# A batch attention with its next group's scores issued a step sooner, its reciprocals kept in the queries' PSUM bank, and VectorE's work in each step put in another order

## The chip, the cores and the metric

The kernel runs on one core of a Trainium2 chip. The metric is the device time of one execution in microseconds (us). All data are float32. The engines are named as in the profile: PE is TensorE (matmuls), DVE VectorE, ACT ScalarE, POOL GpSimd and SP SyncE, which here issues DMAs only. Each engine works through its own instructions in order; semaphores order the engines among themselves.

## What is computed

Two transformer-like layers over x of 16 batches, 512 tokens, 128 features. Layer 0 is a linear attention and a token-shift feed-forward, layer 1 a retention and then the block that the change is in:

```python
def _mha(x, Wqkv, bqkv, Wo, bo):          # S = 16 (batches), B = 512 (tokens)
    qkv = x @ Wqkv.T + bqkv               # 4 heads of 32
    scores = einsum('bhqd,bhkd->bhqk', q, k) * (1.0 / sqrt(hd))
    att = softmax(scores, axis=-1)
    o = einsum('bhqk,bhkd->bhqd', att, v)
    return o.transpose(2, 0, 1, 3).reshape(S, B, D) @ Wo.T + bo

def _moe(x, Wg, W1, b1, W2, b2):          # 8 experts, 128 -> 512 -> 128
    idx = argmax(xf @ Wg.T, axis=-1)
    ...
y = _layer_norm(x + _mha(x, Wqkv, bqkv, Wo, bo), g1, be1)
z = _layer_norm(y + _moe(y, Wg, W1, b1, W2, b2), g2, be2)
```

The attention runs across the 16 batches, for each of the 512 token positions by itself. A token then goes to the one expert of eight whose logit is largest.

## The kernel before

`kernel` calls `build`, which runs six stages one after the other: `prologue`, `attention` (layer 0), `token_shift_ffn`, `attention` (layer 1), `attend_and_route` and `run_experts`. A stage is a block with one program for each engine, and a stage begins when the one before has ended on all engines. The change is in `attend_and_route` alone. There the 8192 rows are 16 groups g of 4 tiles of 128 rows (`G` = 16). Every engine runs `step(s)` for s from -4 to 20 (`run`), written out in full, and in a step each engine works on groups at different stages. The work of a group g:

- ACT normalises it (`act_xn`, in step g-4), POOL scales and shifts it (`pool_scale`, `pool_h`, step g-4) and adds a bias for the residual (`pool_xb`, step g-3), three instructions on 128x512 each. PE transposes it (`pe_T`, step g-3) and ACT brings that to SBUF (`act_hT`).
- PE makes queries, keys and values (`pe_qk`, `pe_v`, step g-2), into the PSUM banks `pq`, `pk` and part of `rows_ps`. ACT takes them out (`act_q`, `act_k`, `act_v`). SP sends the keys to a layout by heads (`sp_kx`, four DMAs).
- `pe_scores` (step g) puts the scores into the bank `pS`: first a mask (L1320), then 32 small matmuls (L1327). DVE takes the maximum (`vec_max`, L1334), subtracts it (`vec_shift`, L1339), ACT makes the exponential (`act_exp`, L1345, in its step behind `act_q` and `act_k` of group g+2), and DVE sums it (`vec_total`, L1350), makes reciprocals (`vec_reciprocal`, L1357), multiplies (`vec_probs`, L1362) and transposes in blocks (`vec_transpose`, L1369, tile `pc`). The reciprocals `rc` are the first 16 columns of `pS`, and the routing's scratch (`lg`, `first`) lies in `pS` too: so `pe_scores(g)` waits for the probabilities of g-1 (`pn_ready`) and for routing.
- SP sends the transposed probabilities to another layout (`sp_ax`, four DMAs into `ax`). In step g+1 PE makes the values' sums (`pe_values`, L1388, bank `pO`), ACT takes them out (`act_o`), and PE multiplies by the output weights (`pe_out`, L1405, in `rows_ps`).
- In step g+2 DVE adds the residual (`vec_u`, L1414) and takes the router's logits (`vec_logits`, L1421), then statistics of the rows (`vec_stats`: four L1429 and the copy L1430 of 128x4 place numbers) and `vec_var` (four L1437).
- In every even step 2r+4 DVE chooses the experts of two groups (`vec_choose`, L1459 to L1468), PE ranks them (`pe_rank`, end of its step), and in step 2r+5 DVE makes the rows' addresses (`vec_dest`, L1485 to L1494). In step g+5 POOL scatters the group's rows by address (`pool_row`, four indirect DMAs, L1512), and it needs these addresses for that.

The order of an engine's step is written out by hand in `pe_step`, `act_step`, `vec_step` and `pool_step`. Before the change, PE's step s is: scores(s), queries, keys and values of s+2, values(s-1), transposition of s+3, out(s-1), ranking. DVE's step s is: rows and logits, statistics of s-2, addresses (odd steps), maximum and subtraction of s, `vec_var`, some statistics of x in the first steps, choice (even steps), then sum, reciprocals, probabilities and transposition of s. In the last steps (s of 12 and more) POOL has no more groups to prepare, and `pool_step` places waits between its rows: for scores(s), for values(s-1) and for out(s-1). Below, "scores(g)", "values(g)", "out(g)" stand for `pe_scores`, `pe_values`, `pe_out` of group g. The functions as they are, with the line numbers of the profile:

## Time and profile before

| what | us |
|---|---|
| median of 3 runs | 1056.25 |
| lowest, highest of them | 1048.0, 1058.28 |
| the profiled execution | 1047.97 |
| its span in the trace | 1046.2 |
| PE, DVE, POOL, ACT, PEld busy in the span | 860.2, 867.7, 721.6, 631.7, 618.0 |

The trace covers one execution. Its span leaves 1.8 us of the device time outside. PEld is the loading of weights, which lies beside PE's matmuls. `attend_and_route` takes from about 684 us of the span to about 875. A row of a timeline gives the start, the duration of the merged instructions, the engine, the line and operation, output and inputs, the count, and in brackets how long the engine was idle before it and what ended that. A window gives the busy time of each engine in a stretch.

### The profile page before, as it was taken

What the parts mean: (1) busy time and instruction counts of PE and PEld (TensorE: products, weight loads), DVE (VectorE), ACT (ScalarE), POOL (GpSimd) and SP (SyncE); (2) the same over time, 40 slices, a digit from 0 to 9 for tenths busy, and PEclk for the clock granted to TensorE, in tenths of its full rate; (3) what the DMA queues carried; (4) which work ended last, traced back from release to release, by engine and by line L of the source; (5) the groups of instructions that cost most, each with busy time, mean ns of one, the idle gap of its engine ahead of it and who ended that gap; (6) DMA issues with size and microseconds to landing.
All of it is one profiled execution on the core that took longest, in us unless ns stands there. A gap on an engine that the chain in (4) does not pass through costs nothing. (4 is left out here: it accounts for less than half of the span.)

```text
span 1046.2 us, 25423 instructions
## 1 busy us (share of the span) xinstructions
PE 860.2 (82%) x5240; PEld 618.0 (59%) x5240; DVE 867.7 (83%) x2853; ACT 631.7 (60%) x1636; POOL 721.6 (69%) x626
## 2 busy tenths in 40 slices
PE   5799999999968867989898989558888732999993
PEld 5466666666636644555555555335555532999993
DVE  5589999999976976989898989778899761899995
ACT  2555555555438956676767675467665202999992
POOL 4488888888852218999999999665598461355554
PEclk9899999999989989999999999869999755999997
DMA  9520000000000000000000000254576664544420
GB/s 245 164 69 1 0 0 0 0 0 0 1 4 1 0 1 1 11 20 10 20 10 20 10 20 10 67 153 110 158 213 205 186 221 124 146 129 132 133 65 20
DMA packets 64935, 70.11 MB, mean 67 GB/s; under 512 B 8965, under 2 KB 52178, under 8 KB 64740
## 3 DMA queue, kind: packets, MB, share of 16 engines
q1 hardware_dynamic: 50612, 47.20, 16.2%
q0 software_dynamic: 6368, 16.89, 4.7%
q10 hardware_dynamic: 7872, 5.08, 1.8%
q8 instruction: 32, 0.52, 0.2%
q14 instruction: 51, 0.42, 0.1%
HBM read 32.32 MB, written 24.50 MB: 54 GB/s over the span
## 5 line engine op out<-in xcount | busy, mean ns | idle before, releaser
L473 PE MATMUL a_pS<-a_kv,utri 128*128 128x360 f32 (+3 forms) x768 | 264.9, 481 | 19.4 <-POOL a_kv L464 9.7
L464 POOL TENSOR_TENSOR a_kv<-a_qk,a_vv 128x1152 f32<-128x1152 f32 (+1 forms) x128 | 264.2, 2065 | 12.6 <-DVE a_qk L438 12.6
L473 PEld LDWEIGHTS a_pS<-a_kv,utri 128*128 128x128 f32 x768 | 136.3, 191 | 100.8 <-issue 25.3
L569 POOL TENSOR_TENSOR a_tt<-a_tt 128x576 f32<-128x576 f32 (+1 forms) x128 | 156.9, 1226 | 49.9 <-DVE a_tt L553 46.0
L553 DVE TENSOR_TENSOR a_tt<-a_pS,a_qk 128x360 f32<-128x360 f32 (+3 forms) x384 | 181.0, 526 | 11.3 <-PE a_pS L473 8.3
L1930 POOL DMA_INDIRECT out_dram<-x_o,x_place x71 | 69.1, 973 | 78.6 <-DVE x_o L1917 75.9
L581 DVE TENSOR_REDUCE a_nd<-a_tt 128x144 f32<-128x720 f32 (+3 forms) x128 | 104.5, 816 | 0.0
L519 ACT ACTIVATE a_tt<-a_pI 128x144 f32<-128x144 f32 (+1 forms) x96 | 40.1, 417 | 105.5 <-PE a_pI L481 105.4
L512 PEld LDWEIGHTS a_pO<-wgate,a_yT 128*128 128x128 f32 x256 | 44.8, 193 | 75.2 <-issue 36.6
L1512 POOL DMA_INDIRECT ys<-m_S,m_dest x64 | 63.0, 984 | 36.8 <-issue 12.3
L512 PE MATMUL a_pO<-wgate,a_yT 128*128 (+1 forms) x256 | 54.7, 296 | 30.8 <-POOL a_yT L543 22.6
L1868 PE MATMUL x_pZ<-w,x_hT 128*128 x568 | 76.9, 279 | 1.4 <-issue 1.3
L1819 ACT ACTIVATE x_w<-w 128x644 f32 x71 | 52.4, 741 | 31.3 <-PEq L1651 26.3
L1868 PEld LDWEIGHTS x_pZ<-w,x_hT 128*128 128x128 f32 x568 | 69.9, 194 | 2.1 <-issue 1.9
L410 ACT ACTIVATE a_vv<-a_pQ 128x128 f32<-128x128 f32 x122 | 33.8, 277 | 55.3 <-PE a_pQ L401 53.4
L372 ACT ACTIVATE a_xn<-X,nmr,rstd 128x128 f32 (+1 forms) x128 | 60.9, 485 | 2.0 <-DVE nmr L275 1.8
L287 DVE BATCH_NORM_STATS2 bn<-X 128x6 f32<-128x128 f32 (+1 forms) x256 | 57.4, 278 | 1.1 <-DMA X<-xs 0.9
L401 PE MATMUL a_pQ<-W,a_hT 128*128 128x384 f32 x122 | 51.5, 504 | 4.2 <-ACT a_hT L388 2.7
L456 POOL TENSOR_TENSOR a_qk<-a_ra,a_rb 128x256 f32<-128x256 f32 x64 | 47.0, 735 | 8.7 <-DVE a_rb L449 8.7
L401 PE MATMUL a_pQ<-wqkv,a_hT 128*128 128x384 f32 x122 | 50.3, 494 | 1.5 <-ACT a_hT L388 1.5
L481 PEld LDWEIGHTS a_pI<-a_R,a_qT 128*128 128x128 f32 x192 | 34.4, 189 | 28.4 <-ACT a_qT L525 11.3
L1850 ACT ACTIVATE x_hT<-x_pA,x_w 128x128 f32<-128x128 f32 x142 | 43.9, 362 | 9.4 <-PE x_pB L1842 9.4
(298 smaller groups left out, 2192.8 us busy)
## 6 DMA issues: line engine op xcount, KB each, us to landing
x_yl<-ys SPq DMA_DIRECT2D x71, 193.5 KB, 2.4
X<-xs SPq DMA_DIRECT2D x16, 256.0 KB, 5.4
kx<-m_kc SPq DMA_DIRECT2D x64, 64.0 KB
ax<-m_pc SPq DMA_DIRECT2D x64, 64.0 KB
m_S<-X SPq DMA_DIRECT2D x16, 256.0 KB, 3.1
xs<-X SPq DMA_DIRECT2D x15, 256.0 KB
w<-in_L_ffn_W_dram SPq DMA_DIRECT2D x1, 2048.0 KB
m_S<-gw ACTq DMA_DIRECT2D x6, 256.0 KB, 3.0
```

The costliest lines, as they stand in the source:

```text
L287: v.bn_stats(K.bn[:, ds(n, 1), :].rearrange("p a f -> p (a f)"), x[:, ds(n, 1), :].rearrange("p a f -> p (a f)"))\
L372: act.activation(xn[:, t, :], tile(K.X, 4 * b + t), ACT.Identity, bias=column(K.nmr, 4 * b + t), scale=column(K.rstd, 4 * b + t)).then_inc ...
L401: pe.matmul(bank_of(b, t, start)[:, 0:3 * P], hT[:, t * P:(t + 1) * P], wqkv, start=True, stop=True).then_inc(qkv_ps, 1)
L464: pool.tensor_tensor(kv[:, t % 2, :, :, :], kk.unsqueeze(2).to_broadcast([P, H, J, D]), vv[:, t, :, :].unsqueeze(3).to_broadcast([P, H, J, ...
L473: pe.matmul(pS[c][:, 0:(h1 - h0) * SC], K.utri[:, :], flat[:, h0 * SC:h1 * SC], start=True, stop=True).then_inc(u_done, 1)
L512: pe.matmul(pO[:, 0:P], yT[:, :], tile(K.wgate[:, 0 if layer == 0 else 2, :, :], b), start=True, stop=True).then_inc(proj_ps, 1)
L553: v.tensor_tensor(tt[:, t % 2, h0:h1, :, 0:D], pS[c][:, 0:(h1 - h0) * SC].rearrange("p (h j i) -> p h j i", i=D, j=J), q[:, h0:h1, :].unsq ...
L569: pool.tensor_tensor(tt[:, t % 2, :, :, D // 2:D], tt[:, t % 2, :, :, D // 2:D], tt[:, t % 2, :, :, 0:D // 2], ALU.add).then_inc(half_done, 1)
L581: v.tensor_reduce(nd[:, t % 2, :, :], tt[:, t % 2, :, :, D // 2:rows], AX.X, ALU.add).then_inc(red_done, 1)
L1512: pool.indirect_dma_start(out=A["ys"], out_offset=bass.IndirectOffsetOnAxis(ap=dest[:, g // 2 % 2, at:at + 1], axis=0), in_=S[:, 4 * (g % ...
L1868: mm = pe.matmul(pZ[j % 2][:, 0:P], hT[:, j % 2, c * P:(c + 1) * P], K.w2[:, ds(e, 1), c, :].rearrange("p a f -> p (a f)"), start=(c == 0) ...
L1930: pool.indirect_dma_start(out=token_rows, out_offset=bass.IndirectOffsetOnAxis(ap=place[:, j:j + 1], axis=0), in_=o[:, j % 4, :], in_offse ...
```

## The change

In `attend_and_route`:

- `rc` moves from `pS` to the first 16 columns of `pq`. `pe_qk(g)` waits for `pn_ready` of g-2 (the probabilities of group g-3 made), `pe_scores(g)` for `sm_ready` of g (the subtraction of g-1 done) where it waited for `pn_ready`, and `vec_reciprocal(g)` for the queries up to g+2 to be taken out of `pq`, where it waited for `sm_ready` and `hot_ready`.
- PE issues scores(s+1) in step s, behind the transposition of s+3 and ahead of out(s-1). It issued scores(s) first in step s.
- DVE begins its step with the maximum and subtraction, then rows and logits, then in odd steps (and the first and last ones) statistics, variance and addresses. In the even steps 4 to 14 statistics and variance come last, behind the transposition.
- In POOL's last steps the second row waits for values(s-1), the third for scores(s+1), the fourth for out(s-1) as before.

```diff
--- before.py
+++ after.py
@@ -1146,7 +1146,8 @@
         pv, pU = four(512 - 3 * PE_), four(1024 - PE_)
         pos, sums = rows_ps[:, 0:8 * E].rearrange("p (e n) -> p e n", e=E), rows_ps[:, 8 * E:9 * E]
 
-        rc, lg, first = pS[:, 0:16], pS[:, 64:64 + 8 * E].rearrange("p (n e) -> p n e", e=E), pS[:, 128:136]
+
+        rc, lg, first = pq[:, 0:16], pS[:, 64:64 + 8 * E].rearrange("p (n e) -> p n e", e=E), pS[:, 128:136]
         unit = lambda g: g // 2 if g < G - 2 else g - G // 2 + 1
         groups = lambda r: [2 * r, 2 * r + 1] if r < G // 2 - 1 else [r + G // 2 - 1]
         tiles = lambda r: 4 * len(groups(r))
@@ -1272,6 +1273,7 @@
         def pe_qk(pe, g):
             pe.wait_ge(hT_ready, g + 1)
             wait(pe, q_ready, g)
+            wait(pe, pn_ready, g - 2)
             pe.matmul(pq[:, :], K.W[:, W_FQ, :], hT[:, :], start=True, stop=True).then_inc(q_ps, 1)
             wait(pe, kc_ready, g)
             pe.matmul(pk[:, :], K.W[:, W_FK, :], hT[:, :], start=True, stop=True).then_inc(k_ps, 1)
@@ -1315,7 +1317,7 @@
 
             if g == 0:
                 pe.wait_ge(mask_ready, 1)
-            wait(pe, pn_ready, g)
+            wait(pe, sm_ready, g)
             wait(pe, hot_ready, (g - 3) // 2)
             pe.matmul(pS[:, :], mask[:, 0:P], mask[:, P:].unsqueeze(1).to_broadcast([2, 16, 32]), start=True, stop=False,
                       skip_group_check=True)
@@ -1352,8 +1354,7 @@
         def vec_reciprocal(v, g):
             v.wait_ge(sum_ready, g + 1)
             wait(v, pn_ready, g)
-            v.wait_ge(sm_ready, g + 1)
-            wait(v, hot_ready, (g - 2) // 2)
+            v.wait_ge(q_ready, min(g + 3, G))
             v.reciprocal(rc, sm_sum[:, :]).then_inc(rc_ready, 1)
 
         def vec_probs(v, g):
@@ -1521,8 +1522,6 @@
 
 
         def pe_step(pe, s):
-            if there(s):
-                pe_scores(pe, s)
             if there(s + 2):
                 pe_qk(pe, s + 2)
                 pe_v(pe, s + 2)
@@ -1530,6 +1529,8 @@
                 pe_values(pe, s - 1)
             if there(s + 3):
                 pe_T(pe, s + 3)
+            if there(s + 1):
+                pe_scores(pe, s + 1)
             if there(s - 1):
                 pe_out(pe, s - 1)
             if even(s - 4) and s < G:
@@ -1576,17 +1577,18 @@
 
         def vec_step(v, s, link):
 
-            if there(s - 2):
-                vec_u(v, s - 2)
-                vec_logits(v, s - 2)
-                vec_stats(v, s - 2)
-            if even(s - 5) and s < G:
-                vec_dest(v, link, (s - 5) // 2)
+            late = even(s - 4) and s < G
             if there(s):
                 vec_max(v, s)
                 vec_shift(v, s)
             if there(s - 2):
+                vec_u(v, s - 2)
+                vec_logits(v, s - 2)
+            if there(s - 2) and not late:
+                vec_stats(v, s - 2)
                 vec_var(v, s - 2)
+            if even(s - 5) and s < G:
+                vec_dest(v, link, (s - 5) // 2)
             x_stats(v, s)
             if s in PARTS:
                 v.wait_ge(stats, 4 * (PARTS[s][2] - 2))
@@ -1598,6 +1600,9 @@
                 vec_reciprocal(v, s)
                 vec_probs(v, s)
                 vec_transpose(v, s)
+            if late:
+                vec_stats(v, s - 2)
+                vec_var(v, s - 2)
             if s in PARTS:
                 vec_x_offset(v, *part_of(s))
             if s == G or s == G + 1:
@@ -1612,12 +1617,12 @@
             if s >= G - 4:
                 if there(s - 5):
                     pool_row(pool, s - 5, 0)
-                pool.wait_ge(s_ps, min(s + 1, G))
                 if there(s + 3):
                     pool_xb(pool, s + 3)
                 if there(s - 5):
+                    pool.wait_ge(o_ps, min(s, G))
                     pool_row(pool, s - 5, 1)
-                    pool.wait_ge(o_ps, min(s, G))
+                    pool.wait_ge(s_ps, min(s + 2, G))
                     pool_row(pool, s - 5, 2)
                     pool.wait_ge(w_ps, min(s, G - 1))
                     pool_row(pool, s - 5, 3)
```

## Rows read from the trace of the kernel before

**Rows 1.** Windows of the span: busy us by engine, then TensorE's clock, DMA share, GB/s

```profile
core 0: us, PE busy (x) PEld busy (x) DVE busy (x) ACT busy (x) POOL busy (x), PEclk, DMA share, GB/s
...
745.90:806.90 61.00, 51.52 (x639) 35.44 (x637) 55.07 (x163) 38.61 (x79) 54.96 (x49) 1.00 0.68 205
...
806.90:845.30 38.40, 27.31 (x324) 21.25 (x325) 30.85 (x119) 10.13 (x20) 19.77 (x20) 0.72 0.61 188
```

**Rows 2.** Timeline of POOL: start us, us, what; idle before and its releaser in brackets

```profile
745.87 1.19 POOL L1512 DMA_INDIRECT ys<-m_S,m_dest  x1 [7.64 <-DVE m_dest L1492]
...
760.73 1.28 POOL L1258 TENSOR_TENSOR X<-X,m_gb 128x512 f32<-128x512 f32 x1
...
763.47 0.97 POOL L1512 DMA_INDIRECT ys<-m_S,m_dest  x1 [0.31 <-issue]
...
806.94 0.97 POOL L1512 DMA_INDIRECT ys<-m_S,m_dest  x1 [0.30 <-issue]
...
844.09 0.97 POOL L1512 DMA_INDIRECT ys<-m_S,m_dest  x1 [1.06 <-PE m_pO L1388]
...
865.80 0.97 POOL L1512 DMA_INDIRECT ys<-m_S,m_dest  x1 [0.30 <-issue]
```

**Rows 3.** Timeline of DVE, the odd step 7 and the start of step 8

```profile
759.50 0.65 DVE L1414 TENSOR_TENSOR m_S<-m_rows_ps,m_U 128x512 f32<-128x512 f32 x1
...
760.19 0.87 DVE L1429 BATCH_NORM_STATS2 m_ubn<-m_S 128x6 f32<-128x128 f32 x4
...
760.98 1.07 DVE L1430 COPY m_S<-m_ids 128x4 f32<-128x4 f32 x1
...
761.96 0.25 DVE L1485 TENSOR_TENSOR m_pick<-m_rows_ps,m_hot 128x64 f32<-128x64 f32 x1
...
762.78 0.69 DVE L1334 TENSOR_REDUCE m_mx<-m_pS 128x16 f32<-128x512 f32 x1
...
763.51 0.69 DVE L1339 TENSOR_TENSOR m_sm<-m_pS,m_mx 128x512 f32<-128x512 f32 x1
...
764.90 0.69 DVE L1350 TENSOR_REDUCE m_sum<-m_ex 128x16 f32<-128x512 f32 x1 [0.41 <-ACT m_ex L1345]
...
766.63 0.71 DVE L1369 STREAM_TRANSPOSE m_pc<-m_pn 128x512 f32<-128x512 f32 x1
...
767.27 0.66 DVE L1414 TENSOR_TENSOR m_S<-m_rows_ps,m_U 128x512 f32<-128x512 f32 x1
```

**Rows 4.** Timeline of DVE, part of the even step 6

```profile
754.60 0.37 DVE L1437 BATCH_NORM_AGGREGATE m_umv<-m_ubn 128x2 f32<-128x6 f32 x4
...
754.88 0.14 DVE L1459 SCALAR_TENSOR_TENSOR m_S<-m_umv,m_S 128x8 f32<-128x8 f32 x1
...
757.16 0.65 DVE L1350 TENSOR_REDUCE m_sum<-m_ex 128x16 f32<-128x512 f32 x1
```

**Rows 5.** Timeline of DVE, steps 1, 2 and 5, and the last group's transposition

```profile
709.75 0.69 DVE L1334 TENSOR_REDUCE m_mx<-m_pS 128x16 f32<-128x512 f32 x1 [0.77 <-PE m_pS L1327]
...
716.82 0.69 DVE L1414 TENSOR_TENSOR m_S<-m_rows_ps,m_U 128x512 f32<-128x512 f32 x1 [1.51 <-PE m_rows_ps L1405]
...
744.12 0.15 DVE L1430 COPY m_S<-m_ids 128x4 f32<-128x4 f32 x1
...
744.72 0.17 DVE L1492 CAST m_dest<-m_posf 128x8 uint32<-128x8 f32 x1
...
836.68 0.71 DVE L1369 STREAM_TRANSPOSE m_pc<-m_pn 128x512 f32<-128x512 f32 x1
```

**Rows 6.** Timeline of PE, steps 1 and 2, and the values of groups 11 and 15

```profile
713.70 1.08 PE L1388 MATMUL m_pO<-ax,m_v 128*32 128x128 f32 x32 [1.18 <-DMA ax<-m_pc]
...
714.71 0.66 PE L1264 MATMUL m_pT<-ident,m_U 128*128 128x128 f32 x4
...
716.72 0.39 PE L1320 MATMUL m_pS<-m_mask 2*128 2x512 bf16 x1
...
717.03 1.08 PE L1327 MATMUL m_pS<-kx,m_qT 128*32 128x128 f32 x32
...
808.98 1.08 PE L1388 MATMUL m_pO<-ax,m_v 128*32 128x128 f32 x32 [2.85 <-DMA ax<-m_pc]
...
841.32 1.94 PE L1388 MATMUL m_pO<-ax,m_v 128*32 128x128 f32 x32 [0.59 <-DMA ax<-m_pc]
```

## The prediction, as put on record

> **What bounds the kernel now.** I read the windows first, to see which engine fills each part of the stage. From 745.9 to 806.9 us POOL is busy 54.96 of 61.00 us, PE 51.52 and DVE 55.07; from 806.9 to 845.3 POOL is busy 19.77 of 38.40, PE 27.31, DVE 30.85, and TensorE's clock falls to 0.72 [rows 1]. Then I read POOL's timeline. Its first scattered row comes at 745.87, after 7.64 us of waiting for addresses. From there to its step 12 at 806.94 it waits for nothing but its own 0.3 us between instructions: 61.07 us for seven steps, 8.72 each [rows 2]. At the end it runs rows back to back, from 844.09 to 865.80 eighteen of them, 1.277 us apart, and the first of the eighteen had waited for values(15) [rows 2]. The last row at 865.80 ends the stage; nothing behind it is changed, so a us gained there is a us of the whole.
>
> So three terms make up the stage: when POOL starts (DVE's steps 0 to 5), seven steps at POOL's rate, and a tail in which POOL waits for PE, and PE for the probabilities. DVE's timeline shows the middle. Step 7 runs from 759.50 to 767.27; in it the place copy takes 1.07 us and ends at 762.05, just when POOL's instruction that began at 760.73 ends (762.01), and there is 0.41 us of idle before the sum [rows 2, 3]. DVE is held by POOL there and not the other way round.
>
> **Part 1: the new order of DVE, steps 0 to 5.** In step 1 DVE waits 0.77 us for scores(1) [rows 5]. Scores(1) now stand at the end of PE's step 0 and only need the subtraction of group 0, so this wait goes. In step 2 DVE waits 1.51 us, until 716.82 [rows 5]. Now the maximum comes first in the step and needs scores(2), which stand behind values(0) and the transposition of group 4: values(0) start at 713.70 when their DMA has landed, the transposition at 714.71 for 0.66, then 0.31 for the mask and 1.08 for the scores [rows 6]: 713.70 + 1.01 + 0.66 + 1.40 = 716.8. The next late thing comes at the same moment, and the 0.77 us is swallowed: 0 gained, at most 0.8.
> Steps 2 to 4 hold the same instructions in another order, so step 5 starts where it did. The first addresses are cast at 744.72 + 0.17, and POOL starts 0.98 later [rows 2, 5]. In the new order maximum, subtraction and variance stand ahead of the addresses in step 5: 0.73 + 0.61 + 0.28 = 1.6 us [rows 3, 4] (0.61 is the subtraction's 0.69 less the 0.08 by which a successor that needs nothing of it overlaps; the variance is from 754.60 to 754.88). Bounds: 0.9 (1.6 less the 0.8) and 2.1 (0.5 more of waiting for POOL). I take 1.2: POOL starts 1.2 us **later**.
>
> **Part 2: the middle.** One DVE step without its waits, from the starts in rows 3 and 4: row and logits 0.69, statistics 0.79, copy 0.08 (0.15 with its overlap, when it does not wait [rows 5]), maximum and subtraction 1.34, variance 0.28, addresses 0.82, sum to the end of the transposition 767.27 - 764.90 = 2.37, choice 757.16 - 754.88 = 2.28. An odd step is 6.4, an even one 7.85 us, 14.2 a pair; POOL takes 17.4 for two steps [rows 2]. The 3.2 us between is spent in waits for POOL before and after. So nothing is gained here: POOL hides it. Exp's round trip (763.51 to 764.90, 1.39 us, of which 0.78 is beyond the subtraction [rows 3]) is now filled with rows and logits, and that too is hidden. What can be lost: in an odd step the addresses follow the copy, now with the variance (0.28) in between. Today the cast ends 0.8 before POOL's row at 763.47, which had waited 0.31 by its own pace [rows 2, 3]; it is just in time. If the copy stays locked to the end of that POOL instruction, steps 7, 9 and 11 each lose 0.28, 0.8 in all; if DVE runs further ahead, 0. I take 0.3. POOL reaches step 12 at 806.94 + 1.5 = 808.4.
> The copy waits whole for POOL's instruction in this trace. The Trainium skill, SBUF — State Buffer, section "SBUF: two separate sides", adds the other direction: a two-port copy of DVE that starts first makes POOL's descriptor writing wait. An estimate by that rule would be the copy's 0.15 us for each of the seven steps in which POOL is full, 1 us slower in all. No row of this trace shows a POOL instruction drawn out by a copy, and the sum does without it.
>
> **Part 3: the waits moved on PE and the bank of the reciprocals.** `pe_qk` of group s+2 now waits for the probabilities of s-1, and behind it stand keys, values, transposition, scores(s+1) and out(s-1). It is the moment for which scores(s) waited at the same place of PE's queue, so PE's step begins no later: 0. The reciprocals wait for the queries of s+2 to be taken out; ACT does that ahead of the exponential, which the sum before them needs anyway: 0. SP's key DMAs can go 1.4 us sooner (scores no longer ahead of the keys), ahead of `sp_ax`: 0, at best a little. Scores(s+1) now wait for the DMA of the probabilities through values(s-1). The longest such wait here is 2.85 us, before values(11) at 808.98 [rows 6]. Before, rows and logits, first in DVE's step, hung on the same values through out(s-1): the chain is as long as it was.
>
> **Part 4: the tail.** DVE's times, from POOL's. In step 11 the addresses are due 0.8 before POOL's row. POOL's step 11 starts at 808.4 - 8.7 = 799.7, so the cast ends at 798.9; it lies 3.9 us (0.73 + 0.61 + 0.69 + 0.79 + 0.08 + 0.28 + 0.71) and about 1 us of waiting into the step. Step 11 starts at 794.0, step 12 at 794.0 + 6.4 + 1 = 801.5. Step 12 is even and still meets POOL's long instructions: 7.85 + 1.3 = step 13 at 810.7. From here only rows are left on POOL, and no long wait: step 14 at 817.1, step 15 at 824.9, the transposition of group 15 ends 6.4 later, 831.3. Before, it ends at 836.68 + 0.71 = 837.39, and values(15) begin at 841.32, 3.93 later [rows 5, 6]. Now 835.2. At the slow clock they take 1.94 [rows 6], and POOL's row comes 0.83 behind them (844.09 against 843.26): 838.0. The new pacing lets one more row wait for values(15): the second of group 11 and not the third, so nineteen rows follow where eighteen did. Last row: 838.0 + 18 x 1.277 = 861.0, against 865.80: **4.8 us sooner** in the tail, the later start of POOL already inside.
> Does another thing come first? Scores(14) hang on the transposition of group 12 (809.5, as the late statistics stand behind it): + 3.9 + 1.0 + 1.4 = 815.8, under 817.1. Scores(15): 817.1 + 6.3 = 823.4, under 824.9. POOL's addresses of step 15: 824.9 + 3.9 + 0.8 = 829.6, and 23 gaps more give 859.0, 2.0 under the forecast. Scores(13) come through values(11): if their DMA takes 6.9 us as now, they are done at 811.5, which is 0.8 later than step 13 as worked out. That makes 4.0 to 4.8; I take 4.5.
> Sum, against the profiled execution (span 1046.2 and 1.8 outside): 1047.97 - 4.5 = 1043.5. That execution lies at the low end of the runs; against their median, 1056.25, it is 1051.7. A tail of full clock would give 0.9 more.
>
> **The rivals.**
> *No change:* the tail's DMAs set the pace. If each probabilities' DMA takes near 6.9 us, as before values(11) [rows 6], in place of 3.9, a tail step costs as much as now, and only the later start is left against the shorter exp wait: 1047 to 1048.5, median 1056. For it: PE is idle 11 of 38 us there. Against: values(15) landed in 3.9.
> *A packed tail:* POOL never waits from step 12 on. Last row = 808.4 + 1.4 (the one long instruction left) + 35 x 1.277 = 854.5, 11.3 sooner: 1036.7, median 1045. Against: the addresses of step 15 alone give 859.0.
> *Slower:* POOL's late start with no tail to pay for it. POOL starts 2.1 late, steps 7, 9, 11 lose 0.8, the nineteenth row 1.3: 4.2 slower, 1052.2, median 1060.5. It decides from the point where the addresses, now 1.6 deeper in DVE's odd steps, come later than POOL's own pace of 8.7 in every pair; each further us of port wait ahead of them then costs 1 us for each of four pairs, and 10 us if DVE's pair passes 19.5. Against: 14.2 of work against 17.4.
>
> **How the numbers follow.** Forecast (gain of 2 to 8, by the median 1048 to 1054) 0.60, no change 0.17, packed 0.12, slower 0.11. Runs differ by 10 us among themselves, so about 1% is what a measurement here can tell from no change. Over 1% faster: the packed tail, and 0.04 for a median that falls at the low level: 0.16. Over 1% slower: 0.04 of the slower case. Within 1%: 0.80. Range: from 1043 (the low level less 5, or most of the packed tail) to 1058 (no change, or a little slower).
>
> **What would show it.** Right: DVE's wait of 0.77 gone, POOL's first row at about 747, steps of 8.7 up to about 808.4, values(15) near 835, nineteen rows behind them, the last near 861. Wrong: a step of POOL above 8.9 between 747 and 808; a first row before 745.9; waits of DVE for scores above 1 us in steps 13 to 15; a last row behind 864 or before 857.

## The result, and the profile after

The changed kernel takes 1058.39 us in the median of 16 runs (1054.82 to 1058.98), the kernel before 1049.46 in the median of 16 (1046.81 to 1058.28). The ratio is 1.0076, with a 95% interval of 1.0060 to 1.0091: slower by 0.8%, where 0.4% faster was forecast. The profiled execution took 1056.54 us against 1047.97. The median of 1056.25 that the prediction started from rests on three executions of the kernel before; its 16 executions here have 1049.46.

First a window of the changed kernel, with the columns of [rows 1]:

```profile
745.90:806.90 61.00, 44.08 (x518) 30.18 (x510) 51.18 (x137) 33.68 (x68) 46.50 (x42) 0.94 0.60 178
```

In the stretch in which POOL was full (54.96 us) it is now busy 46.50, PE 44.08 where it was 51.52, and TensorE's granted clock is 0.94 where it was 1.00. The instructions are the same ones as before, so fewer of them fall into this stretch: somebody waits. POOL's timeline of the changed kernel, against [rows 2]:

```profile
745.23 1.18 POOL L1513 DMA_INDIRECT ys<-m_S,m_dest  x1 [8.47 <-DVE m_dest L1493]
...
760.07 1.29 POOL L1259 TENSOR_TENSOR X<-X,m_gb 128x512 f32<-128x512 f32 x1
...
766.31 0.97 POOL L1513 DMA_INDIRECT ys<-m_S,m_dest  x1 [3.79 <-DVE m_dest L1493]
...
775.00 0.97 POOL L1513 DMA_INDIRECT ys<-m_S,m_dest  x1 [0.31 <-issue]
...
780.92 1.29 POOL L1259 TENSOR_TENSOR X<-X,m_gb 128x512 f32<-128x512 f32 x1
...
787.16 0.97 POOL L1513 DMA_INDIRECT ys<-m_S,m_dest  x1 [3.79 <-DVE m_dest L1493]
...
808.05 0.97 POOL L1513 DMA_INDIRECT ys<-m_S,m_dest  x1 [3.80 <-DVE m_dest L1493]
...
816.75 0.98 POOL L1513 DMA_INDIRECT ys<-m_S,m_dest  x1 [0.30 <-issue]
...
852.48 0.97 POOL L1513 DMA_INDIRECT ys<-m_S,m_dest  x1 [2.50 <-PE m_pO L1389]
...
875.47 0.97 POOL L1513 DMA_INDIRECT ys<-m_S,m_dest  x1 [0.30 <-issue]
```

POOL's first row is at 745.23. Then it waits 3.79, 3.79 and 3.80 us for addresses (`m_dest`) at the start of steps 7, 9 and 11. From step 7 to 9 it takes 20.85 us, from 9 to 11 20.89, where two steps took 17.4. VectorE's timeline of one such pair, the odd step 7 and the even step 8, with the copy ahead of it (against [rows 3, 4]):

```profile
759.60 1.81 DVE L1431 COPY m_S<-m_ids 128x4 f32<-128x4 f32 x1
...
761.61 0.65 DVE L1336 TENSOR_REDUCE m_mx<-m_pS 128x16 f32<-128x512 f32 x1
...
764.82 0.23 DVE L1486 TENSOR_TENSOR m_pick<-m_rows_ps,m_hot 128x64 f32<-128x64 f32 x1
...
765.34 0.17 DVE L1493 CAST m_dest<-m_posf 128x8 uint32<-128x8 f32 x1
...
770.76 0.69 DVE L1336 TENSOR_REDUCE m_mx<-m_pS 128x16 f32<-128x512 f32 x1 [2.69 <-PE m_pS L1329]
...
772.78 0.80 DVE L1460 SCALAR_TENSOR_TENSOR m_S<-m_umv,m_S 128x8 f32<-128x8 f32 x1
...
775.39 2.04 DVE L1469 TENSOR_TENSOR_SCAN m_upto<-m_reset,m_hot 128x72 f32<-128x72 f32 x1
...
780.45 1.80 DVE L1431 COPY m_S<-m_ids 128x4 f32<-128x4 f32 x1
...
782.46 0.65 DVE L1336 TENSOR_REDUCE m_mx<-m_pS 128x16 f32<-128x512 f32 x1
```

And PE's in step 7 and at the end of step 8, with values(15) as the last line (against [rows 6]):

```profile
765.30 1.16 PE L1288 MATMUL m_rows_ps<-wv,m_hT 128*128 128x136 f32 x8 [2.33 <-DVE m_pick L1486]
...
766.40 1.08 PE L1389 MATMUL m_pO<-ax,m_v 128*32 128x128 f32 x32
...
767.41 0.66 PE L1265 MATMUL m_pT<-ident,m_U 128*128 128x128 f32 x4
...
768.31 1.08 PE L1329 MATMUL m_pS<-kx,m_qT 128*32 128x128 f32 x32
...
777.59 0.37 PE L1322 MATMUL m_pS<-m_mask 2*128 2x512 bf16 x1 [1.85 <-DVE m_upto L1469]
...
849.71 1.93 PE L1389 MATMUL m_pO<-ax,m_v 128*32 128x128 f32 x32 [1.03 <-DMA ax<-m_pc]
```

What the reader is to see: in step 7 PE's `pe_v` (L1288) waits 2.33 us for `m_pick`, the first instruction of the addresses (L1486). It starts at 765.30, when that instruction (764.82 + 0.23) has ended. Values(6), the transposition and scores(8) follow it in the queue, and VectorE's step 8 waits 2.69 us, until 770.76, where the profile names these scores. Their record ends at 769.39 (768.31 + 1.08), and what fills the last 1.37 us no view shows; in steps 10 and 12, with waits of 2.92 and 2.37, the maximum comes less than 0.1 behind the scores' end. In step 8 three of VectorE's instructions are drawn out: L1460 to 0.80 us, the scan L1469 to 2.04 and the place copy to 1.80.

The time can be split at a few marks. They are VectorE's first maximum of this stage (704.41 before, 702.63 after), POOL's first row, POOL's step 12, its last row and the span's end:

| stretch | before | after | difference |
|---|---|---|---|
| start to first maximum | 704.41 | 702.63 | -1.8 |
| to POOL's first row | 41.46 | 42.60 | +1.1 |
| to POOL's step 12 | 61.07 | 71.52 | +10.5 |
| to POOL's last row | 58.86 | 58.72 | -0.1 |
| to the end of the span | 180.40 | 179.23 | -1.2 |

The sum is 8.5 us, the difference of the spans. The middle, which was forecast to cost 0.3, costs 10.5, and the tail, forecast to give some 6 back from POOL's step 12 on, gives nothing.

### The profile page after: what moved, and what is told of

Its sections match the earlier page's. It is cut to its first block and busy times, and to the rows that moved or that the text cites. A ratio compares the mean times of both kernels' runs of the same rounds, so it can differ in the third digit from the quotient of the medians.

```text
span 1054.7 us, 25405 instructions
## 1 busy us (share of the span) xinstructions
PE 860.8 (82%) x5240; PEld 617.6 (59%) x5240; DVE 871.4 (83%) x2853; ACT 631.3 (60%) x1636; POOL 721.6 (68%) x626
## 3 DMA queue, kind: packets, MB, share of 16 engines
q1 hardware_dynamic: 50612, 47.20, 16.4%
## 5 line engine op out<-in xcount | busy, mean ns | idle before, releaser
L473 PE MATMUL a_pS<-a_kv,utri 128*128 128x360 f32 (+3 forms) x768 | 263.2, 479 | 18.2 <-POOL a_kv L464 8.3
L512 PE MATMUL a_pO<-wgate,a_yT 128*128 (+1 forms) x256 | 54.7, 296 | 30.9 <-POOL a_yT L543 22.5
```

Source lines behind the costliest of these rows:

```text
L473: pe.matmul(pS[c][:, 0:(h1 - h0) * SC], K.utri[:, :], flat[:, h0 * SC:h1 * SC], start=True, stop=True).then_inc(u_done, 1)
L512: pe.matmul(pO[:, 0:P], yT[:, :], tile(K.wgate[:, 0 if layer == 0 else 2, :, :], b), start=True, stop=True).then_inc(proj_ps, 1)
```

## The experiments

Ratios are against runs of the kernel before on the same chip, and the medians of that kernel moved between the three sets (1045.24, 1045.19, 1049.38), so results are compared by ratio, and a time by itself only with the times expected on the same chip. Most versions ran 10 or 12 times, v_behind and pe_as_before 4 times. The expectations use letters for the theories. A: PE's `pe_v` waits for the addresses' first instruction, because the ranks lie in its bank. B: the addresses come late only through VectorE's own waits for POOL. C: the early scores, which wait for the choice, hold PE. D: the place copy and the addresses behind it are by themselves enough for the loop. E, formed after the second set: A's wait and the waits for POOL together are more than the 3.2 us that VectorE has to spare. Each diff is against the changed kernel where nothing else is said.

**dest_first** moves the addresses to the head of VectorE's step.

```diff
+            if even(s - 5) and s < G:
+                vec_dest(v, link, (s - 5) // 2)
             if there(s):
                 vec_max(v, s)
...
-            if even(s - 5) and s < G:
-                vec_dest(v, link, (s - 5) // 2)
```

> The changed kernel with the addresses (vec_dest) first in VectorE's odd steps, ahead of the maximum. Theory A (in odd steps pe_v(s+2) waits for the addresses of the same step, because the ranks and the values share the bank, and behind it in PE's queue stand values(s-1), the transposition and scores(s+1); after the change the addresses come 1.6 us and more later in the step, so PE stands 3.9 us and VectorE 2.4 to 2.9 in each pair of steps): PE's waits for m_pick fall under 0.5 us each, POOL waits under 1 us for addresses in steps 7, 9 and 11 where it now waits 3.8, a pair of steps takes 17.4 to 18.5 us in place of 20.9, time 1046 to 1050. Theory B (VectorE's own port waits, 3.8 us a pair in the scan, the copy and L1460, hold the pair up): pair above 20, time 1055 to 1059. Theory C (the early scores wait for the choice, hot_ready, in even steps): that wait stays, so does the time, 1055 or more.

Measured: ratio 1.0012 (0.9997 to 1.0028), 1047.29 us. POOL's rows at the start of steps 7, 9 and 11:

```profile
762.25 0.97 POOL L1513 DMA_INDIRECT ys<-m_S,m_dest  x1 [0.80 <-DVE m_dest L1493]
...
780.12 0.98 POOL L1513 DMA_INDIRECT ys<-m_S,m_dest  x1 [0.80 <-DVE m_dest L1493]
...
798.70 0.97 POOL L1513 DMA_INDIRECT ys<-m_S,m_dest  x1 [1.47 <-DVE m_dest L1493]
```

POOL waits 0.8, 0.8 and 1.47, and a pair takes 17.87 and 18.58. The loss is gone. That excludes C as a cause of the whole, since the early scores and their wait for the choice are still there. By the figures A is met but for the last pair (18.58 against at most 18.5, a wait of 1.47 against under 1), and B's are missed. Yet the edit does not separate PE's wait from VectorE's waits for POOL: with the addresses at the head, PE's wait for the bank goes, but the addresses also no longer stand behind the copy of their own step and its wait for POOL.

**v_behind** leaves the addresses late and moves `pe_v` behind the scores in PE's step.

```diff
             if there(s + 2):
                 pe_qk(pe, s + 2)
-                pe_v(pe, s + 2)
...
             if there(s + 1):
                 pe_scores(pe, s + 1)
+            if there(s + 2):
+                pe_v(pe, s + 2)
```

> The changed kernel with pe_v(s+2) issued behind scores(s+1) in PE's step, and nothing else. Theory A: the addresses stay late and pe_v still waits for them, but nothing urgent stands behind it; VectorE's waits for scores at the start of even steps (2.4 to 2.9 us) fall under 1, pair 17.4 to 18.5, time 1046 to 1051. Theory B: pair above 20, time 1055 or more. Theory C: scores(s+1) wait for the choice as before, time 1055 or more.

Measured: ratio 1.0211 (1.0182 to 1.0240), 1067.39 us: slower still than the changed kernel. A had said 1046 to 1051; "1055 or more", which B and C had said, holds, but not for their reasons. Three of the long waits of the stretch from 745 to 817 us (total, times, longest):

```profile
ACT m_v L1314 <- PE m_rows_ps L1288: 29.3, 6, 6.6
...
DVE m_S L1415 <- PE m_rows_ps L1406: 8.1, 6, 2.2
...
POOL ys L1513 <- DVE m_dest L1493: 21.2, 4, 7.7
```

The experiment made a wait of its own. In ScalarE's step the values (`act_v`) stand ahead of `act_o`, `act_hT` and the next group's normalisation; with late values all of these are late, out(s-1) too, and VectorE waits 8.1 us for its rows. VectorE's long waits for scores did go (0.5 us in all), as A had said, but the two pairs took 20.9 and 22.8 us. So A's figures failed, and with the new wait beside it the run decides nothing about A's cause, but it shows once more that an instruction moved back in one queue has to be followed into the next.

**pe_as_before** has PE's order, and POOL's waits of the last steps, of the kernel before: VectorE's new order and the bank alone.

```diff
+            if there(s):
+                pe_scores(pe, s)
             if there(s + 2):
                 pe_qk(pe, s + 2)
                 pe_v(pe, s + 2)
...
-            if there(s + 1):
-                pe_scores(pe, s + 1)
```

> The changed kernel with PE's order and POOL's waits of the last steps as in the kernel before (scores(s) first in step s): VectorE's new order and the bank of the reciprocals alone. Theory A: pe_v(s+2) still waits for late addresses and scores(s+1) still stand behind it, now behind out(s-1) too: no better than the changed kernel, 1055 to 1062. Theory C: scores no longer wait for the choice, and the time falls to 1050 or less. Theory B: the port waits stay, 1055 or more.

Measured: ratio 1.0137 (1.0112 to 1.0162), 1060.13 us, slower than the changed kernel.

The longest waits of this kernel from 745 to 817 us:

```profile
PE m_rows_ps L1288 <- DVE m_pick L1486: 13.8, 4, 4.5
...
DVE m_mx L1336 <- PE m_pS L1329: 16.4, 4, 4.4
```

POOL's timeline at the start of its steps 7 and 9:

```profile
767.55 0.98 POOL L1513 DMA_INDIRECT ys<-m_S,m_dest  x1 [3.78 <-DVE m_dest L1493]
...
788.44 0.97 POOL L1513 DMA_INDIRECT ys<-m_S,m_dest  x1 [3.79 <-DVE m_dest L1493]
```

The waits are A's, longer than in the changed kernel: 13.8 us of PE for `m_pick` (there 10.1), 16.4 of VectorE for scores (there 10.5), and the pair is 20.89 again. C, which had said 1050 or less, falls: the early scores are no cause of the loss, and without them it is larger.

**vec_as_before** is the other half: VectorE's order of the kernel before, PE's new order and the bank.

```diff
-            late = even(s - 4) and s < G
+            if there(s - 2):
+                vec_u(v, s - 2)
+                vec_logits(v, s - 2)
+                vec_stats(v, s - 2)
+            if even(s - 5) and s < G:
+                vec_dest(v, link, (s - 5) // 2)
             if there(s):
                 vec_max(v, s)
                 vec_shift(v, s)
...
```

> The changed kernel with VectorE's order of the kernel before: PE's new order and the bank of the reciprocals alone. Theory A: the addresses are early again, pe_v waits 0.3 us for them, pair 17.4 to 18, time 1046 to 1050. Theory B: the port waits go back to 2.9 us a pair, also 1046 to 1050. Theory C: scores(s+1) still wait for the choice of step s (which in this order comes 0.8 us and more later), time above 1054.

Measured: ratio 1.0035 (1.0020 to 1.0050), 1049.27 us. PE's wait for the ranks' reader from 745 to 817 us, and POOL's rows at the start of steps 7 and 12:

```profile
PE m_rows_ps L1288 <- DVE m_pick L1486: 0.8, 2, 0.4
...
765.64 0.97 POOL L1513 DMA_INDIRECT ys<-m_S,m_dest  x1 [1.90 <-DVE m_dest L1493]
...
809.13 0.98 POOL L1513 DMA_INDIRECT ys<-m_S,m_dest  x1 [0.31 <-issue]
```

PE waits 0.8 us in all for `m_pick`. POOL still waits once, 1.90 us ahead of step 7; from there to step 12 it takes 43.5 us for five steps, its own pace. So most of the loss comes from VectorE's order. What is left, 0.35% slower, shows no gain from early scores by themselves.

**pick_first** tells PE's wait from POOL's. Only the instruction that reads the ranks, and so frees their bank for `pe_v`, goes ahead; the rest of the addresses stays where the change put it.

```diff
+            if even(s - 5) and s < G:
+                vec_pick(v, (s - 5) // 2)
             if there(s):
                 vec_max(v, s)
...
-                vec_dest(v, link, (s - 5) // 2)
+                vec_dest(v, link, (s - 5) // 2, picked=True)
```

> The changed kernel with only the first instruction of vec_dest (L1486, the one that reads the ranks and frees their bank) moved ahead of the maximum in odd steps; the reduction and the cast that make the addresses stay late. Theory A (PE's wait for the ranks' bank sets the pair): PE's waits of 2.3 to 3.9 us for m_pick go, pair 17.4 to 18.5 us, time 1046 to 1050. Theory D (a loop between VectorE and POOL: the late place copy of an even step waits until POOL's third long instruction of that step ends, then come 4.2 us of VectorE work up to the cast and 0.8 to POOL's row, so the next POOL step starts 3.5 us late): PE's waits go and nothing is gained, pair 20.7 to 20.9, POOL waits 3.6 to 3.8 in steps 7, 9 and 11, time 1055 to 1059.

Measured: ratio 0.9966 (0.9945 to 0.9987), 1042.70 us. By the pace of the middle this is A's outcome (the time lies 3 us below A's range), and it is the one version of the study whose interval lies below the kernel before: faster by 0.1 to 0.6%. It is one such interval of twelve, and the two versions built on it, below, have intervals that reach 1.

POOL's timeline (first row, starts of steps 7, 9, 11 and 12, last row):

```profile
746.17 1.19 POOL L1518 DMA_INDIRECT ys<-m_S,m_dest  x1 [8.47 <-DVE m_dest L1498]
...
763.79 0.97 POOL L1518 DMA_INDIRECT ys<-m_S,m_dest  x1 [0.31 <-issue]
...
781.17 0.97 POOL L1518 DMA_INDIRECT ys<-m_S,m_dest  x1 [0.30 <-issue]
...
798.57 0.98 POOL L1518 DMA_INDIRECT ys<-m_S,m_dest  x1 [0.30 <-issue]
...
807.28 0.97 POOL L1518 DMA_INDIRECT ys<-m_S,m_dest  x1 [0.31 <-issue]
...
864.85 0.97 POOL L1518 DMA_INDIRECT ys<-m_S,m_dest  x1 [0.30 <-issue]
```

PE's timeline at `pe_v` of step 7:

```profile
759.97 1.16 PE L1288 MATMUL m_rows_ps<-wv,m_hT 128*128 128x136 f32 x8 [0.65 <-DVE m_S L1415]
```

`pe_v` waits 0.65 us, and not for the ranks. POOL is back at 17.4 us a pair with nothing but its own 0.3 us between instructions. D, which held that the late copy and the addresses behind it are enough for the loop, falls in that form: copy and cast stand as late in VectorE's list as before this edit. What has moved is when they come. The late copy of step 8 now starts at 774.20, 1.7 us behind POOL's row of that step, and is free again at 774.79; in the changed kernel it started 5.45 us behind that row and waited for POOL's third long instruction. Here the copy of step 9 meets that instruction and ends at 779.74; the cast is done at 780.33, 0.8 ahead of POOL's row at its own pace (781.17).

**copy_on_act** takes the place copy away from VectorE; ScalarE makes it for group s-2, behind `act_hT` in its step.

```diff
-            v.tensor_copy(S[:, ring(g), TO], ids[:, 4 * g:4 * g + 4]).then_inc(place_done, 1)
...
+        def act_place(act, g):
+            if g == 0:
+                act.wait_ge(tab_in, 5 * 16)
+            if g >= RG:
+                act.wait_ge(rows_out[g % RG], 64 * (g // RG))
+            act.activation(S[:, ring(g), TO], ids[:, 4 * g:4 * g + 4], ACT.Copy).then_inc(place_done, 1)
...
+            if there(s - 2):
+                act_place(act, s - 2)
```

> The changed kernel with the place copy made by ScalarE at the end of its step, VectorE's order otherwise unchanged. Theory D: without the lock at the copy the next one behind it in the loop decides, the scan's (its end follows POOL's first long instruction of the even step); from its end to the cast lie 7.4 us, so the pair falls to 19 to 19.5 and the time to 1049 to 1054. Theory A: PE still waits for the late addresses, pair 20.5 or more, time 1056 or more.

Measured: ratio 1.0023 (0.9996 to 1.0050), 1049.21 us.

The longest waits from 745 to 817 us:

```profile
PE m_rows_ps L1288 <- DVE m_pick L1492: 9.3, 5, 2.3
...
DVE m_mx L1336 <- PE m_pS L1329: 4.4, 4, 1.7
```

POOL's timeline at the start of its steps 8 and 10:

```profile
773.28 0.97 POOL L1519 DMA_INDIRECT ys<-m_S,m_dest  x1 [0.30 <-issue]
...
790.66 0.97 POOL L1519 DMA_INDIRECT ys<-m_S,m_dest  x1 [0.30 <-issue]
```

PE still waits 9.3 us in all for `m_pick` (10.1 in the changed kernel), the longest of them 2.3 and not 3.9; yet the pair is 17.38. A alone would have kept 20.5, D 19 to 19.5 (its time, 1049 to 1054, is met at the edge). By the pair both failed as single causes. The edit did not leave the rest as it was, though: VectorE's waits for scores fell too, from 10.5 to 4.4 us, and its waits for POOL went to other instructions (the cast of step 9 takes 1.39 us, 779.15 to 780.54, where POOL's third long instruction ends at 780.50). There is a second caution. The profiled execution took 1043.92 us; four of the ten executions lie between 1041.98 and 1044.94, the other six between 1048.72 and 1050.59. The trace shows the faster sort, and what the pair is in the slower one, whose times lie at D's lower edge, no trace shows. From these rows theory E was formed: the bank's wait and the waits for POOL together are more than VectorE has to spare, and taking either away is enough.

**not_late** has statistics, copy and variance of the even steps ahead of the choice.

```diff
-            late = even(s - 4) and s < G
+            late = False
```

> The changed kernel with statistics and variance of the even steps ahead of the choice (late is False), so that the even steps' place copy comes in the middle of the step. Theory E: the wait for the ranks' bank stays as it is (addresses as deep in the odd step), VectorE's sum per pair is 14.2 + 2.7 + the waits for POOL; those fall from 3.8 to 2 to 3 us or move, so a pair of 19 to 20.9, time 1049 to 1058. Theory D (only the late copy makes the loop): pair 17.4 to 18, time 1046 to 1049.

Measured: ratio 0.9986 (0.9962 to 1.0010), 1048.67 us. E had said a pair of 19 to 20.9 and 1049 to 1058, D a pair of 17.4 to 18 and 1046 to 1049: the time lies inside D's range and just outside E's.

VectorE's timeline in step 8 (maximum, copy, scan):

```profile
768.02 0.69 DVE L1336 TENSOR_REDUCE m_mx<-m_pS 128x16 f32<-128x512 f32 x1 [2.36 <-PE m_pS L1329]
...
770.86 0.32 DVE L1431 COPY m_S<-m_ids 128x4 f32<-128x4 f32 x1
...
773.33 1.72 DVE L1469 TENSOR_TENSOR_SCAN m_upto<-m_reset,m_hot 128x72 f32<-128x72 f32 x1
```

POOL's timeline at the start of its steps 7, 9 and 11:

```profile
763.91 0.97 POOL L1513 DMA_INDIRECT ys<-m_S,m_dest  x1 [1.02 <-issue]
...
782.02 0.97 POOL L1513 DMA_INDIRECT ys<-m_S,m_dest  x1 [1.02 <-issue]
...
800.17 0.97 POOL L1513 DMA_INDIRECT ys<-m_S,m_dest  x1 [1.03 <-issue]
```

The pair takes 18.1, and POOL waits 1.0 at the odd steps. In step 8 VectorE waits 2.36 us where it waited 2.69, the scan still takes 1.72, but the copy is down to 0.32. The bank's wait shrank as well: PE stands 1.15 us before `pe_v` of step 7, not 2.33, and VectorE's waits for scores from 745 to 817 us add up to 7.5, not 10.5. So E's figure failed: with two of its parts still there, the pair is 0.1 above D's range and 0.9 under E's. What E and D share stands, that the late copy's wait is needed; that the waits simply add up against VectorE's 3.2 us to spare is not borne out.

**dest_first_act**, **pick_first_act** and **dest_first_act_early** combine edits already shown: dest_first with copy_on_act, pick_first with copy_on_act, and dest_first with copy_on_act and not_late.

> dest_first (addresses first in VectorE's odd steps) and the place copy on ScalarE. Theory D: no copy's lock stands ahead of the addresses any more, POOL waits no more than 0.3 us from its first row up to step 12 (dest_first: 0.8 twice and 1.5), pair 17.4, time 1 to 4 us under dest_first's. Theory A: PE's waits as in dest_first, time as dest_first's within 1 us.

Measured: ratio 0.9998 (0.9978 to 1.0019), 1044.34 us; dest_first had 1.0012 (0.9997 to 1.0028). POOL keeps its own pace, 17.4 us a pair, as D had said. The intervals overlap, so D's gain of 1 to 4 us is not shown.

> As dest_first_act, with statistics and variance of the even steps ahead of the choice again (late is False). Both theories: the pair stays at 17.4; the probabilities of even steps come 1 us later, so a tail as fast as dest_first_act's or 0 to 1 us slower. If the late statistics cost something of their own, 1 to 3 us faster.

Measured: ratio 0.9981 (0.9953 to 1.0009), 1044.55 us, not to be told from dest_first_act.

> pick_first and copy_on_act together. Theory E (each undoes the 3.5 us a pair of steps by itself: the ranks' bank makes VectorE wait 2.4 to 2.9 us a pair, and with 3.8 us of waits for POOL, in the scan, the place copy and L1460, that is more than the 3.2 us which VectorE has to spare against POOL): the middle is at POOL's pace with either, so the two together are no more than 2 us faster than pick_first, and no slower. If the two costs added up independently, it would be 6 us or more faster than pick_first.

Measured: ratio 0.9982 (0.9958 to 1.0007), where pick_first has 0.9966 (0.9945 to 0.9987). Together they are no faster than one alone; that the costs add up independently (6 us, 0.6% more) is excluded.

**bank_alone** is the kernel before with the reciprocals in `pq` and the changed waits, all orders as before. Against the kernel before:

```diff
-        rc, lg, first = pS[:, 0:16], pS[:, 64:64 + 8 * E].rearrange("p (n e) -> p n e", e=E), pS[:, 128:136]
+        rc, lg, first = pq[:, 0:16], pS[:, 64:64 + 8 * E].rearrange("p (n e) -> p n e", e=E), pS[:, 128:136]
...
             wait(pe, q_ready, g)
+            wait(pe, pn_ready, g - 2)
...
-            wait(pe, pn_ready, g)
+            wait(pe, sm_ready, g)
...
-            v.wait_ge(sm_ready, g + 1)
-            wait(v, hot_ready, (g - 2) // 2)
+            v.wait_ge(q_ready, min(g + 3, G))
```

> The kernel before with the reciprocals in the queries' bank and the waits that go with it, all orders as before. Theory E and the prediction alike: no wait of length is added or removed in the middle, time within 2 us of the kernel before. If the wait of the queries' matmul for the probabilities costs something, 1 us for each of 14 steps at most.

Measured: ratio 1.0004 (0.9979 to 1.0029). No cost of the bank and its waits can be told, as the prediction's part 3 said.

**pick_first_pace** gives pick_first the `pool_step` of the kernel before, with the waits that its last steps had there (scores(s) ahead of the rows, values(s-1) ahead of the third).

```diff
                 if there(s - 5):
                     pool_row(pool, s - 5, 0)
+                pool.wait_ge(s_ps, min(s + 1, G))
                 if there(s + 3):
                     pool_xb(pool, s + 3)
                 if there(s - 5):
+                    pool_row(pool, s - 5, 1)
                     pool.wait_ge(o_ps, min(s, G))
-                    pool_row(pool, s - 5, 1)
-                    pool.wait_ge(s_ps, min(s + 2, G))
                     pool_row(pool, s - 5, 2)
```

> pick_first with POOL's waits of the last steps as in the kernel before. The third row and not the second of group 11 waits for values(15): 18 rows behind it in place of 19, so 1.3 us faster than pick_first if values(15) decide the end, 0 if the addresses do.

Measured: ratio 0.9986 (0.9958 to 1.0013), against 0.9966 (0.9945 to 0.9987). No gain from one row fewer behind values(15) can be told; whether the new pacing is worth anything stays open.

## Why the prediction was wrong, step by step

**The failed step: part 3, with part 2 resting on it.** The prediction said of PE that its step begins no later, and priced the queue behind `pe_qk` at 0. It listed what stands behind `pe_qk`, but not the waits of `pe_v`, which stands among it. That has four waits, and one of them, `pos_read` of (g-5)//2, is for the first address instruction of the same odd step, because the ranks lie in the bank into which the values of group s+2 go. Before, that instruction came 2.5 us into VectorE's step (759.50 to 761.96 [rows 3]), and now it comes 3.2 us in (761.61 to 764.82), behind the maximum and the subtraction; and the step as a whole begins later, because the maximum of each even step waits for scores that stand behind the `pe_v` of the odd step before it. The 1.6 us by which the addresses moved were priced for POOL alone. What stood in the place of the 0 is PE's wait of 2.33 us in step 7 and 3.90 in steps 9 and 11, and the middle of the stage 10.5 us longer, where 0.3 was forecast. Runs that show it: pick_first (one instruction moved, 1.0076 to 0.9966) and pe_as_before (the wait without the early scores, 1.0137).

**The second half: part 2's slack.** The prediction's measure of VectorE was right: 14.2 us of work a pair against 17.4 for POOL, 3.2 to spare. It took the waits for POOL as what fills this gap and said "nothing is gained here: POOL hides it". That holds only if these waits shrink when VectorE falls behind. They do not. Against the 17.4 stand, in the pair from 761.61 to 782.46 of the changed kernel:

| part of VectorE's pair | us |
|---|---|
| work | 14.2 |
| wait before the maximum, for scores | 2.7 |
| L1460 beyond the 0.14 of [rows 4] | 0.7 |
| scan beyond the 0.3 that it takes when POOL has only rows | 1.7 |
| place copy beyond its 0.15 | 1.65 |
| sum | 20.95 |

The pair is 20.85. The table is an account of where the time lies: its parts add up to the pair whatever the cause, so it proves none. In the kernel before, the scan took 0.40 and L1459 0.14 in these steps, and only the two copies waited. Delayed by the bank's wait, VectorE meets POOL's three long instructions at other places of its list, and at three instead of two. The pattern then repeats itself, because POOL's next step waits for VectorE: from 759.60 the copy waits until 761.4, when POOL's instruction that began at 760.07 (1.29 us) has ended; 4.1 us later the cast is done (765.34 + 0.17), and 0.8 later POOL's row starts (766.31).

Once round this loop gives the pair to the hundredth. POOL's step 7 takes 8.69 us (766.31 to 775.00); 7.21 later its third long instruction of step 8 ends (780.92 + 1.29); the late copy ends at 782.25; 4.1 later the cast is done (786.36) and 0.8 later POOL's row starts (787.16): 20.85. PE is not a link of it. Its wait is the condition: it holds VectorE back by so much that the late copy comes where POOL's third long instruction stands. pick_first takes the condition away, copy_on_act and not_late the copy at that place, and each brings the pair back to 17.4 to 18.2. That is theory D's loop with A's wait as what keeps it closed, and it fits these traces better than E's sum. Shown is that each of the three edits ends the loss; that the phases lock in just this way is read from one trace of each kernel and was not varied finely, and for copy_on_act that trace is one of the faster sort.

**Right.** POOL's first row was forecast 1.2 us later, and is 1.1 later against the first maximum. (In the span's time that row is at 745.23, ahead of the 745.9 that was named as a sign of being wrong, because the stage began 1.8 us sooner.) VectorE's step 1 has lost its 0.77 us of wait. In step 2 the maximum comes at 716.16, 13.53 us behind the first one; before, step 2 began 12.41 behind it (716.82). Forecast was no difference; PE's granted clock was 0.62 from 711.5 to 716 us, and scores(2) took 1.92 us where 1.08 was assumed. Yet step 5 began 0.5 us sooner than before against the first maximum (37.7 against 38.2), since from step 2 to step 4 the place copies and the choice waited 1.6 us less for POOL. So the size of part 1 is right in part by luck: two errors of 1.1 and 1.6 us, neither of them foreseen, leave 0.5, about the 0.4 that the forecast took off the 1.6 of the addresses. The bank shows no cost (bank_alone). Nineteen rows follow values(15), 22.99 us from the first to the last (852.48 to 875.47), as forecast.

**The tail**, forecast at 52.6 us from POOL's step 12 to the last row, took 58.7. Its working began with VectorE 6.9 us ahead of POOL at step 12 (801.5 against 808.4). It was 4.0 ahead (812.71 against 816.75), for it had lost its lead in the middle. In pick_first, where the lead is 6.5 us (800.75 against 807.28), the tail takes 57.6, still 5.0 over the forecast. So there the sizes of part 4 were wrong too. PE's timeline of pick_first at values(13), scores, out, and at values(15):

```profile
820.98 1.93 PE L1389 MATMUL m_pO<-ax,m_v 128*32 128x128 f32 x32 [4.21 <-DMA ax<-m_pc]
...
823.38 1.94 PE L1329 MATMUL m_pS<-kx,m_qT 128*32 128x128 f32 x32
...
825.25 2.18 PE L1406 MATMUL m_rows_ps<-wo,m_oT 128*128 128x136 f32 x8
...
839.09 1.94 PE L1389 MATMUL m_pO<-ax,m_v 128*32 128x128 f32 x32 [1.16 <-DMA ax<-m_pc]
```

Values(13) start 4.85 us behind the end of the transposition of group 13 (815.42 + 0.71), and not 3.9, after 4.21 us in which PE stood. The granted clock is 1.00 from 812 to 816 us, 0.79 from 816 to 821, where PE is busy 0.79 of 5 us, and 0.50 from 821 to 827.5: values, scores and out then take 1.93, 1.94 and 2.18 where about 1.08 was assumed for the first two. In copy_on_act the tail took 54.7 us (808.02 to 862.72), nearer the forecast; this is one execution each.

**The rivals.** The slower case named the place (the addresses, now deeper in the odd steps) and a size of 1 us for each us of waiting ahead of them, but priced the port's waits and not PE's, and so put 4.2 us and a chance of 0.11 on it. Its condition "if DVE's pair passes 19.5" is what happened, and the 10 us that it named for that case are near the 10.5 of the middle; the pair was not expected to get there, with 14.2 of work against 17.4. The sign of being wrong that it gave, a step of POOL above 8.9, came in steps 6, 8 and 10 (12.2 us each).

## What to carry to other kernels

When an instruction moves back in one engine's step, look up every semaphore that it raises and every wait on it in the other programs, not only the consumer for which it is made: here a bank shared by two tenants made the moved instruction the gate of PE's queue. Where one engine waits out instructions of another, as VectorE does POOL's here, these waits do not fill idle time for free: a new wait elsewhere shifts the phase, and both can grow together. And if a reorder goes wrong, try freeing the shared thing first (one instruction, -1.1% here) before the order is given up.

## What the runs showed of the hardware

VectorE's scan of 128x72 (two operands in SBUF) took 0.31 us with POOL idle or issuing rows, and 2.04 to 2.06 in the steps 6, 8, 10 and 12. In step 8 it began at 775.39; POOL's instruction on 128x512 began at 775.98 and ended at 777.26, and the scan ended at 777.43. The Trainium skill, SBUF — State Buffer, section "Who interferes with whom", says that a VectorE instruction with two SBUF inputs contends with a GpSimd instruction that reads SBUF, and that the one which issues first holds the port. The first half agrees with this trace. The second is not seen here: the scan's record begins 0.6 us ahead of POOL's, and yet it waited (POOL's spans are rough, so the order of issue is not certain).

In the prediction a rule of another section of this page of the Trainium skill, "SBUF: two separate sides", stood for a slowing of POOL by VectorE's copies, 1 us in all by its estimate. No run shows it: POOL's seven steps from its first row to step 12 take 61.11 us with the place copies on VectorE (pick_first) and 61.07 with them on ScalarE (copy_on_act).

The wait of PE costs twice where it is long: in the changed kernel PE stood 3.90 us before `pe_v` at 786.16, and behind it the granted clock was 0.66 from 786.2 to 790.5 us; values took 1.65 us and a transposition 1.12, where 1.08 and 0.66 are usual. Behind the 2.33 us before `pe_v` at 765.30 both had their usual length.
